# Leading the last stage of a two-layer kernel into the stage before it, and adding its routed rows four tiles ahead

## Reference, cut to what matters

```python
t = t + _L1_ffn_ref(_ln_t(t), w_router, w1_stack, w2_stack, ws1, ws2)
# inside, for the normalised tokens h (4096 x 256):
sh = square(relu(einsum('btc,fc->btf', h, ws1)))        # shared branch, 512 hidden
shared_out = einsum('btf,cf->btc', sh, ws2)
inter = square(relu(binned @ w1[e]))                    # routed branch, 8 experts, 256 hidden
outb  = inter @ w2[e]                                   # two experts for each token
moe_out[token] += weight * outb[row of the token]
return shared_out + moe_out
```

## Time and profile before

| | us |
|---|---|
| median of 3 runs | 1146.46 (1141.75 to 1146.63) |
| the profiled execution's own time | 1144.96 |
| its span | 1143.2 |
| second experts' stage, first gather to last copy | 888.5 to 1036.3 |
| last stage, first load to the end of the span | 1038.4 to 1143.2 |

### The profile page before, as it was taken

One profiled execution on the slowest core, in us unless ns is written; L12 is line 12 of the kernel. 1 busy time (PEld: TensorE's weight loads), 2 busy tenths in 40 slices (PEclk: granted clock), 3 DMA queues, 4 the chain that ended last, 5 costly groups with the idle time before them and its releaser, 6 DMA issues. The chain is left out here.

```text
span 1143.2 us, 19741 instructions
## 1 busy us (share of the span) xinstructions
PE 995.9 (87%) x5614; PEld 808.7 (71%) x5614; DVE 616.8 (54%) x1713; ACT 530.7 (46%) x1344; POOL 267.5 (23%) x274
## 2 busy tenths in 40 slices
PE   6857579999999999991689999999775799996998
PEld 2843468888888888881566666666535699995997
DVE  6887733223322332325746677555778355553776
ACT  6536444434444443433344343433235466665773
POOL 0000021111111111105742200000000444432676
PEclk9558669999999999995799999998665799998999
DMA  9544311111111111106532201002230344444554
GB/s 383 232 148 175 120 35 54 52 56 51 52 56 56 51 52 56 52 28 214 160 117 65 87 1 56 38 19 74 102 120 1 90 137 136 139 129 138 175 163 143
DMA packets 63235, 114.68 MB, mean 100 GB/s; under 512 B 9698, under 2 KB 43124, under 8 KB 62132
## 3 DMA queue, kind: packets, MB, share of 16 engines
q1 hardware_dynamic: 49908, 77.72, 19.3%
q0 software_dynamic: 12960, 35.41, 10.8%
q10 hardware_dynamic: 288, 0.47, 0.1%
HBM read 73.96 MB, written 39.59 MB: 99 GB/s over the span
## 5 line engine op out<-in xcount | busy, mean ns | idle before, releaser
L600 POOL DMA_INDIRECT experts_rows_sb<-h_rows,choices x142 | 134.3, 946 | 729.6 <-POOLq L428 400.0
L787 DVE TENSOR_TENSOR experts_a_sb<-experts_a_sb,experts_bankU 128x512 f32<-128x512 f32 x71 | 48.9, 689 | 225.4 <-PE experts_bankU L183 225.4
L740 ACT ACTIVATE experts_a_sb<-experts_bankG 128x512 f32<-128x512 f32 (+1 forms) x142 | 69.6, 490 | 93.5 <-PE experts_bankG L183 93.5
L731 ACT ACTIVATE experts_hT<-experts_bankH 128x256 fp32r<-128x256 f32 x142 | 54.2, 382 | 90.4 <-PE experts_bankH L660 90.3
L753 ACT ACTIVATE experts_y_sb<-experts_bankY 128x256 f32<-128x256 f32 x142 | 54.6, 384 | 87.3 <-PE experts_bankY L180 66.8
L1161 POOL DMA_INDIRECT attn_y<-y_rows,choices x64 | 65.3, 1021 | 92.7 <-POOLq L120 38.1
L181 PE MATMUL attn_bankC<-attn_padded,attn_w_high 128*128 128x512 f32 x144 | 68.1, 473 | 16.1 <-ACT attn_feat L1447 13.9
L860 POOL DMA_INDIRECT shared_y<-y_rows,choices x64 | 67.7, 1057 | 47.6 <-DVE x_res L969 21.1
L180 PE MATMUL experts_bankY<-down_plain,experts_aT_plain 128*128 x284 | 73.0, 379 | 0.0
L186 DVE TENSOR_TENSOR experts_aT<-experts_bankA,experts_aT 128x256 fp32r<-128x256 f32 x142 | 59.7, 420 | 23.9 <-ACT experts_aT L748 23.9
L667 PE MATMUL experts_bankA<-konst_sb,experts_a_sb 128*128 128x128 f32 x426 | 70.1, 274 | 0.4 <-DVE experts_aT L186 0.4
(11 more groups left out here) (370 smaller groups left out, 2755.6 us busy)
## 6 DMA issues: line engine op xcount, KB each, us to landing
y_rows<-experts_y_sb SPq DMA_DIRECT2D x142, 128.0 KB, 1.7
h_rows<-xn SPq DMA_DIRECT2D x32, 256.0 KB, 2.1
mix_xT<-in_xt SPq DMA_DIRECT2D x4, 1024.0 KB, 12.5
x_res<-in_x SPq DMA_DIRECT2D x4, 1024.0 KB, 14.4
gate_raw<-in_L_ffn_gate_w SPq DMA_DIRECT2D x2, 2048.0 KB, 12.9
up_raw<-in_L_ffn_up_w SPq DMA_DIRECT2D x1, 4096.0 KB, 24.8
x_rows<-x_res SPq DMA_DIRECT2D x16, 256.0 KB, 2.6
x_res<-x_rows SPq DMA_DIRECT2D x8, 512.0 KB, 4.7
```

What stands on the lines that cost most here:

```text
L600: nc.gpsimd.indirect_dma_start(rows[t % DEPTH][:, :], None, h_dram, bass.IndirectOffsetOnAxis(ap=ids_i[:, t:t + 1], axis=0)).then_inc(s_ro ...
L740: nc.scalar.activation(a_sb[i % RING][:, :], bankG[i % RING][:, 0:hidden], ACT.Silu if gate is not None else ACT.Relu).then_inc(s["act"], 1)
L787: nc.vector.tensor_tensor(a_sb[i % RING][:, :], a_sb[i % RING][:, :], bankU[i % RING][:, 0:hidden], ALU.mult).then_inc(s["a"], 1)
```

## The change

The objects of the shared stage that concern its turned rows (two raw buffers, two split pairs, two of the four `bankU` PSUM banks and their semaphores) move into a class `SharedLead`, which is made before the second experts' stage and lives through both. `mlp` gets a parameter `follow`.

- SP issues the loads of groups 0 and 1 at the beginning of the experts' stage.
- ACT and DVE split group 0 at the end of their step for slot tile 69 and group 1 at the end of their step for slot tile 70.
- PE makes the products c = 0 and c = 1 after its last `project_back`.
- The last stage starts with products 2 to 5, and ACT's and DVE's orders there start at c = 0 with no split before.
- DVE adds routed rows four tiles ahead (AHEAD_Y = 4), the first from low_a(2) on, and in the loop behind low_a.

```diff
@@ mlp, SP, before the first store
+                        if follow is not None:
+                            for g in range(RING):
+                                follow.load(sp, g)
@@ mlp, PE, behind the last project_back
+                    if follow is not None:
+                        for c in range(follow.EARLY):      # EARLY = 2
+                            follow.project(pe, c)
@@ mlp, end of ACT's step
+                        if follow is not None and not ahead:
+                            follow.high_h(act, t - (n_tiles - AHEAD))
@@ mlp, end of DVE's step
+                        if follow is not None and not ahead:
+                            follow.low_h(dve, t - (n_tiles - AHEAD))
@@ SharedLead
+                self.bankU = [pb(f"shared_bankU{k}", self.N, on=on) for k in range(self.EARLY)]
+            def load(self, sp, g): ...          # bodies as in shared before
+            def high_h(self, act, g): ...
+            def low_h(self, dve, g): ...
+            def project(self, pe, c): ...
@@ shared
+                bankU = lead.bankU
+                bankU.extend(pb(f"shared_bankU{k}", N, on=on) for k in range(lead.EARLY, KI))
@@ shared, SP
-                    for g in range(2 * RING):
-                        load(g)
+                    for g in range(RING, 2 * RING):
+                        lead.load(sp, g)
@@ shared, PE
-                    for c in range(LEAD):
-                        project(c)
+                    for c in range(lead.EARLY, LEAD):
+                        lead.project(pe, c)
@@ shared, ACT
-                    high_h(0)
-                    high_h(1)
@@ shared, DVE
-                    low_h(0)
-                    low_h(1)
                     for c in range(LEAD):
                         low_a(c)
+                        if c >= LEAD - AHEAD_Y:
+                            add_routed(c - LEAD + AHEAD_Y)
                         if c == KI - 1:
-                            low_h(RING)
-                    add_routed(0)
+                            lead.low_h(dve, RING)
                     for t in range(TILES):
-                        add_routed(t + 1)
                         add_y(t)
                         c = t + LEAD
                         low_a(c)
+                        add_routed(t + AHEAD_Y)
                         if c % KI == KI - 1:
-                            low_h(c // KI + RING)
+                            lead.low_h(dve, c // KI + RING)
```

More of the change, by code:

```diff
@@ L543, in _, with mlp @@
                     nc.vector.tensor_copy(experts_i[:, :], words_ps[0:1, 0:WORDS])
-        def mlp(tag, n_tiles, hidden, up, down, gate=None, load=(), experts=True, sink=None, plain=None):
+        def mlp(tag, n_tiles, hidden, up, down, gate=None, load=(), experts=True, sink=None, plain=None, follow=None):
             KI = hidden // P
@@ L830, in _ @@
                         add_y(n_tiles - 1, n_tiles - 1)
-        def shared(ws1, ws2):
+        class SharedLead:
             GROUP = 4
@@ L836, in shared, with __init__ @@
             KI = IS // P
+            N = GROUP * P
+            EARLY = 2
+            def __init__(self, ws1, on):
+                self.ws1 = ws1
+                self.s = {n: sem(f"shared_{n}") for n in ("h_high", "h_low", "up", "relu")}
+                self.s_raw = [sem(f"shared_raw{b}") for b in range(RING)]
+                self.hT_raw = [sb(f"shared_hT_raw{b}", [P, KC * self.N], on=on) for b in range(RING)]
+                self.hT = [[sb(f"shared_hT{b}_{part}", [P, KC * self.N], HALF, on=on) for part in range(2)] for b in range(RING)]
+                self.bankU = [pb(f"shared_bankU{k}", self.N, on=on) for k in range(self.EARLY)]
@@ new lines, in load, with high_h @@
+            def load(self, sp, g):
+                if g >= self.GROUPS:
+                    return
+                if g >= RING:
+                    sp.wait_ge(self.s["h_low"], g - RING + 1)
+                width = KC * self.N
+                sp.dma_start(self.hT_raw[g % RING][:, :], ht_dram[:, g * width:(g + 1) * width]).then_inc(self.s_raw[g % RING], 16)
+            def high_h(self, act, g):
+                if g >= self.GROUPS:
+                    return
+                act.wait_ge(self.s_raw[g % RING], (g // RING + 1) * 16)
+                if g >= RING:
+                    act.wait_ge(self.s["up"], (g - RING + 1) * self.KI)
+                nc.scalar.activation(self.hT[g % RING][0][:, :], self.hT_raw[g % RING][:, :], ACT.Copy).then_inc(self.s["h_high"], 1)
@@ new lines, in low_h, with project @@
+            def low_h(self, dve, g):
+                if g >= self.GROUPS:
+                    return
+                dve.wait_ge(self.s["h_high"], g + 1)
+                low_half(nc.vector, self.hT[g % RING][1][:, :], self.hT_raw[g % RING][:, :], self.hT[g % RING][0][:, :]).then_inc(self.s["h_low"], 1)
+            def project(self, pe, c):
+                g, k = c // self.KI, c % self.KI
+                if g >= self.GROUPS:
+                    return
+                pe.wait_ge(self.s["h_low"], g + 1)
+                if g:
+                    pe.wait_ge(self.s["relu"], c - self.KI + 1)
+                for kc in range(KC):
+                    last = product(self.bankU[k][:, :], [w[:, kc * IS + k * P:kc * IS + (k + 1) * P] for w in self.ws1],
+                                   [x[:, kc * self.N:(kc + 1) * self.N] for x in self.hT[g % RING]], kc == 0, kc == KC - 1)
+                last.then_inc(self.s["up"], 1)
@@ L837, in shared @@
+        def shared(lead, ws2):
+            GROUP, GROUPS, KI, N = lead.GROUP, lead.GROUPS, lead.KI, lead.N
             LEAD = KI + 2
             DEPTH = 8
-            N = GROUP * P
+            AHEAD_Y = DEPTH // 2
             with ExitStack() as on:
-                s = {n: sem(f"shared_{n}") for n in ("h_high", "h_low", "up", "relu", "square", "a_high", "a_low", "down", "sum", "added", "stored")}
-                s_raw = [sem(f"shared_raw{b}") for b in range(RING)]
+                s = dict(lead.s, **{n: sem(f"shared_{n}") for n in ("square", "a_high", "a_low", "down", "sum", "added", "stored")})
@@ L865, in _ @@
                 def _(sp):
[L866 to L871, removed]
-                    for g in range(2 * RING):
-                        load(g)
+                    for g in range(RING, 2 * RING):
+                        lead.load(sp, g)
                     for g in range(GROUPS):
-                        load(g + 2 * RING)
+                        lead.load(sp, g + 2 * RING)
                         for t in range(g * GROUP, (g + 1) * GROUP):
@@ L882, in _ @@
                 def _(pe):
[L884 to L894, removed]
                     def project_back(t):
@@ L905, in project_back @@
                         last.then_inc(s["down"], 1)
-                    for c in range(LEAD):
-                        project(c)
+                    for c in range(lead.EARLY, LEAD):
+                        lead.project(pe, c)
                     for t in range(TILES):
                         project_back(t)
-                        project(t + LEAD)
+                        lead.project(pe, t + LEAD)
                 @block.scalar
                 def _(act):
[L916 to L922, removed]
                     def activate(c):
@@ L941, in _ @@
                         if c % KI == KI - 1:
-                            high_h(c // KI + RING)
+                            lead.high_h(act, c // KI + RING)
                 @block.vector
                 def _(dve):
[L947 to L951, removed]
                     def low_a(c):
@@ L2285, in build @@
             router_tail("moe1", choice, logits1[:, PARTS[1][0] * E:PARTS[1][1] * E])
-        mlp("experts1", SLOT_TILES, I1, up1, down1)
-        shared(ws1, ws2)
+        with ExitStack() as held:
+            lead = SharedLead(ws1, held)
+            mlp("experts1", SLOT_TILES, I1, up1, down1, follow=lead)
+            shared(lead, ws2)
 def padded_pair(v, h, axis):
```

3 lines of the change are left out of this document (removed).

## The result

Median of 7 runs 1138.22 us (1136.92 to 1138.91), against 1145.85 (1141.75 to 1146.66) for the kernel before. The medians differ by 7.6 us. The ratio is 0.9938 with a 95% interval of 0.9924 to 0.9952, which is 7.1 us (5.5 to 8.7). The profiled execution took 1138.44 with a span of 1136.6.

The account below looks back on a forecast made before the run. PE was taken to bound the last stage's middle, the start-up chain its seam and the gathers its last 2.9 us. Gains 6.6 + 2.5 - 1.7 = 7.4 us, so 1144.96 - 7.4 = 1137.6; range 1132 to 1143.

Parts of the forecast that it names:

- (a): Splits in the experts' last tiles: turn_a(70) 1.4 us later, last project_back 1.8 later (bounds 0 to 4.5).
- (b): Products 0 and 1 behind the experts' last project_back: the last stage's block start, s, moves 2.2 us later, to s' = 1040.6.
- (c): Last stage's start: ACT's first relu 0.7 us after s', first project_back (PB0) at 1049.4 instead of 1056.0, gain 6.6.
- (d): PE's pause ahead of the last stage's project_back(0): half clock for 3.4 us follows, costing 1.7 us (bounds 0 and 3.4).
- (e): Last stage, add_routed four tiles ahead: cost 0 at the start (bounds 0 to 0.7), gain 2.5 us at the end.
- rival 1: Last stage: the clock doesn't fall at the pause, or PE hardly pauses; gain 9.1 us, 1135.9; chance 0.17.
- (f): Loads of groups 0 and 1 at the start of the experts' stage, beside the first gathers: cost 0 (bounds 0 to 1).
- Rival 2: Clock falls twice, at the experts' tail pauses and the later pause; gain 5.7 us, 1139.3; chance 0.24.
- rivals 3 and 5: 3: tail splits at upper bound or gather landing, 1140 to 1141, chance 0.10; 5: end's 2.5 missing, 1140.1, chance 0.05.
- Rival 4: Last stage: gathers become the bound and the kernel slower; at 1.60 us per gather, 1151.4; chance 0.04.

Follow-up runs that it names:

- e10: The changed kernel itself, unedited, as a control against the kernel before on the same chip: median 1138.47 us, ratio 0.9945 (0.9924 to 0.9966).
- e5: Changed kernel with the splits moved behind ACT's and DVE's last copy_a of the experts' stage; ratio to the kernel before 0.9931, on a chip with remote waits.
- e7: Changed kernel with the edits of both e5 and e6; ratio to the kernel before 0.9946, on a chip with remote waits.
- e9: Changed kernel with the edits of e5 and e6, and DVE's first add_routed moved behind low_a(3) and low_h(2); 1138.06 us, ratio to the kernel before 0.9943.
- e6: Changed kernel with relu and square of c = 1 and 3 of the first group on DVE; ratio to the kernel before 0.9944, chip with remote waits.

## Why the prediction was right

The forecast was 1137.6 and the median 1138.22. The gain was forecast at 7.4; it is 7.6 by medians, 7.1 by the ratio, and 8.0 in the two aligned traces. The mechanism is the one forecast. That the number is met to 0.6 us is luck: eight executions of the changed kernel on one chip (e10) spread from 1130.42 to 1140.45, the forecast starts from one execution of the kernel before, and the terms were off by up to 0.7 us in both directions, one of them decided by chance.

- (a) Splits in the experts' tail: +1.4 on `turn_a` was +1.8, +1.8 on the last `project_back` was +1.9. Measured from tile 65, over seven traces, both are +1.2 to +1.8. e5, e7 and e9, where both vanish, show the cause.
- (b) s: +2.2 was +2.5, and +1.8 to +2.4 from tile 65.
- (c) ACT's first relu ran 0.03 us after s, not 0.7. PB0 gained 6.9 instead of 6.6. The prediction named ACT as what is late next. e6 and e9 show that DVE with the gathers stood right behind it.
- (d) The clock fell, for 3.4 us, but cost 1.3 and not 1.7. The step's argument was too strong: it took the pauses of one trace for a rule that holds at any place, and gave the other outcome 0.17. At this place it is near one half. (It counted one pause too few: the trace of before has six of 1.9 to 3.5 us that began at full clock, and all six were followed by a fall.) The Trainium skill, "TensorE: Matmul & The Clock Gate", section "HAM oscillation", would have a pause of this length harmless; four executions disagree, five agree.
- (e) The end: 2.5 was 2.5 in the first profile, 1.8 in e10, where the last add is 1.1 behind PE. The size was right, the reason only in part. The prediction puts the gain on the step at which the last gathers are used. But POOL waited for a buffer only once, at gather 8, so what the new order and the lead gave is the shorter wait there, 12 us before and none after. At the start gather 1 landed 4.8 us after its issue, where the median of 3.1 was taken; `add_routed`(0) still ended 0.1 us before `low_a`(3) could start, so the cost was 0. The prediction put the gathers' pace at 1.3 us and the end they allow at s' + 91.4 for 1.36. That bound was right, and it was closer than the text treated it: rival 1, "no fall", forecast 1.7 us more and gave 0.6.
- (f) 0 was 0.

Rival 2 (two falls) did not occur: the pauses of 1.7 and 0.3 in the tail passed at full clock in every profile. Neither did rivals 3 and 5: the splits cost 1.9 and not 4.5, and the 2.5 at the end came. Rival 4 holds as a mechanism at a smaller size: the gathers bind at 1.36 us each as soon as PE keeps its clock (e10), but as a floor near the forecast rather than a loss. Of the prediction's signs, a first `project_back` at s' + 8.9 was 8.2, and the absence of a wait for a gather at the end held in the first profile and not in e10.

## What to carry to other kernels

Loading and splitting the next stage's first inputs inside the stage before is worth the whole start-up chain less what the moved work costs in a tail that is itself a chain; such work costs least behind the last link of the tail (1.4 to 1.5 us here against 1.8 to 2.4 in front of it), though in this kernel the difference never reached the end. When a stage is shortened from its front, work out at once the floor that each other engine sets from its own first instruction (here 64 gathers at 1.36 to 1.39 us): the two edits that took some 2 us more off the front bought nothing. A ring of buffers stands still until its first user runs, so look for the one long wait at the ring's second turn. A wait placed early in an in-order queue, here for a gather, becomes the bound as soon as the work in front of it is made faster.

## What the runs showed of the hardware

- The same pause of 2.3 us on PE was followed by half clock in four of nine profiled executions, each time for 3.4 us at first. Of 90 pauses of 1.5 to 3.0 us at full clock between 200 us and the second experts' stage, over all traces, 87 were followed by it within 2 us.
- On two of three chips ACT and DVE stood still in the last stage for up to 10.8 us at a time, in kernels that ran without such waits on the third chip; the whole program took some 2% longer. The cause is open.
- The first gather of the experts' stage, issued beside 1 MB of loads, landed 4.9 us after its issue, and 2.7 in the kernel before, without the loads.
- POOL issues these indirect gathers of 128 rows at best 1.25 us apart, and 1.36 to 1.39 on average over this stage.
